# Latent attention core: the score banks seeded by ScalarE and VectorE copies in place of TensorE products

## The chip, the cores and the metric

The kernel is a whole four-layer decoder on one core of a Trainium2 chip. The metric is the device time of the program in microseconds, as the median of the runs. The engines are TensorE (PE; its weight loads are PEld), VectorE (DVE), ScalarE (ACT), GpSimd (POOL) and SyncE (SP), which issues the DMAs; each runs its own instructions in the order in which they are written and waits on semaphores.

## The reference, cut to what matters

Of twelve sublayers the change touches one, the latent cross-attention of layer 2. Its queries come from the 512 decoder positions of each of 4 batches, its keys and values from 1024 context positions and those 512 together, in 16 heads of 64.

```python
def _L2_xattn_ref(x, latents, ln_m_g, ln_m_b, ln_l_g, ln_l_b, Wq, Wkv, Wout):
    ...
    q = lat @ Wq
    kv_input = jnp.concatenate([x, lat], axis=1)
    kv = kv_input @ Wkv
    ...
    q, k, v = (split_heads(q), split_heads(k), split_heads(v))
    dots = jnp.einsum('bhid,bhjd->bhij', q, k) * scale
    attn = jax.nn.softmax(dots, axis=-1)
    out = jnp.einsum('bhij,bhjd->bhid', attn, v)
```

The softmax is taken with the row maximum subtracted before the exponential; the maximum comes from products of operands rounded to bf16, and any value near it serves, since it cancels in the division.

## The kernel before

`latent_core_stage` does the attention itself. A group is two heads of one batch, so there are 8 groups in a batch and 32 in all; `for_groups` runs the first two unrolled, then a loop of three turns of eight groups, then the last six. In a group the 1536 keys are cut into 12 tiles of 128 (`nkt`), and a step i works on one tile of keys against all 512 queries of both heads. TensorE's order in a group is written by hand, two steps at a time:

- `scores` for i and for i+1. Each puts, for both heads, a product of a row of ones with the row of negated maxima (L1017, the seed) and then the fp32 product of keys and queries (L1019) into two PSUM banks. The banks from `B0` on are four: two for even steps, two for odd ones, so `scores` of step i waits for the exponential of step i-2.
- one `pass_a` (L999): the rounded bf16 products of the next group, whose maxima VectorE takes (L1123). There are 12 a group, and they run ahead: those that step i issues for the next group are number i+4 on, and the last four belong to the group after it. Their two banks are single, so each waits for VectorE to have read the one before it.
- `weigh` (L1029) for i-2 and i-1: values times exponentials, into the bank `ACC`.
- a second `pass_a`.

`turn` (L1006) transposes the next group's row maxima at i = 8, and `spread` (L1039) sums the last group's totals over the partitions at i = 2. ScalarE takes the exponential of both heads in one instruction of 128x1024 (L1102), copies the sums of the last group after step 1 (L1089) and rounds the operands of the group after next after step 5 (L1082, L1083). VectorE takes the maxima, at i = 8 turns the transposed maxima into two bf16 parts (`negate`: L1132, L1133, L1135), adds a third of one head's exponentials (L1142) and inverts the last group's sums (L1150). GpSimd adds the other exponentials (L1188, L1193) and multiplies by the inverse (L1198). SyncE's queue holds, in each group, a wait for the last group's values products, the load of the next values (L955) and of the operands three groups on (L951, L952), and `row`: a wait for `negate` and four small DMAs that put the parts into the strips of `max_row` (L965).

Of the kernel before, what the change touches and what calls it, by code (L numbers as in the profile page):

```python
# [23 lines left out]
F32 = mybir.dt.float32  # L24
# [7 lines left out]
P = 128  # L32
# [826 lines left out]
def latent_core_stage(k, q_store, k_store, values, nk, scale, att_of):  # L859
# [26 lines left out]
    with ExitStack() as held:  # L886
        def sb(what, shape, dt=F32):
            return held.enter_context(nc.sbuf_tensor(f"lc_{what}", shape, dt))
# [5 lines left out]
        max_row, ones_row = sb("max_row", [P, 2, nq], BF16), sb("ones_row", [P, P], BF16)  # L894
# [4 lines left out]
        negative, max_parts = sb("negative", [SLOTS, P]), sb("max_parts", [SLOTS, ROW_PARTS, P], BF16)  # L899
        (rounded, a_ready, a_taken, row_done, turned, high_made, row_made, row_in, s_ready, exp_done, pv_done, acc_copied,  # L900
         added_by_pool, added_by_vector, sums_ready, inverted, normed, set_up, *more) = held.enter_context(k.stage(
             "rounded", "a_ready", "a_taken", "row_done", "turned", "high_made", "row_made", "row_in", "s_ready", "exp_done", "pv_done",
             "acc_copied", "added_by_pool", "added_by_vector", "sums_ready", "inverted", "normed", "set_up",
# [42 lines left out]
        def _(sync):  # L946
# [11 lines left out]
            def row(b, g):  # L958

                if before(b, g, 1):  # L960
                    sync.wait_ge(set_up, 1)
                sync.wait_ge(row_made, at(b, g, 1, 1))
                for j in range(HEADS):
                    for p in range(ROW_PARTS):
                        sync.dma_start(max_row[j * D + p:j * D + p + 1, g % 2, :].rearrange("o (i t) -> o i t", t=P),  # L965
                                       max_parts[j * nqt:(j + 1) * nqt, p, :]).then_inc(row_in, 16)
# [22 lines left out]
        def _(pe):  # L989
# [18 lines left out]
            def scores(b, g, i):  # L1008

                if i == 0:  # L1010
                    pe.wait_ge(loaded[g % RING], loads_done(b, g))
                    pe.wait_ge(row_in, 16 * HEADS * ROW_PARTS * at(b, g, 1, 1))
                if not (before(b, g, 1) and i < 2):
                    pe.wait_ge(exp_done, at(b, g, nkt, i - 1))
                out = [k.ps[:, B0 + (i % 2) * HEADS + j, 0:nq] for j in range(HEADS)]
                for j in range(HEADS):
                    nc.tensor.matmul(out[j], ones_row[strip(j), :], max_row[strip(j), g % 2, :], start=True, stop=False)  # L1017
                for j in range(HEADS):
                    mm = nc.tensor.matmul(out[j], k_tile[g % RING][strip(j), i * P:(i + 1) * P], q_tile[g % RING][strip(j), :], start=False, stop=True)  # L1019
                mm.then_inc(s_ready, 1)  # L1020
# [12 lines left out]
            def spread(b, g, negated):  # L1033

                pe.wait_ge(row_made, negated)
# [5 lines left out]
                mm.then_inc(sums_ready, 1)  # L1041

            for p in range(NP):
                pass_a(0, 0, p)
# [3 lines left out]
            pe.wait_ge(set_up, 1)  # L1048
# [28 lines left out]
        def _(act):  # L1077
# [12 lines left out]

            round_operands(0, 0)
            round_operands(0, 1)

            def group(b, g):
                for i in range(nkt):
                    if not (before(b, g, 1) and i < TILES):
# [16 lines left out]
        def _(dve):  # L1113
            nc.vector.memset(ones_row[:], 1.0)
            nc.vector.memset(max_row[:], 0.0).then_inc(set_up, 1)

# [11 lines left out]
            def negate(b, g):  # L1128
                dve.wait_ge(turned, at(b, g, 1, 1))
                if not before(b, g, 1):  # L1130
                    dve.wait_ge(row_in, 16 * HEADS * ROW_PARTS * at(b, g, 1, 0))
                nc.vector.tensor_scalar(max_parts[:, 0, :], k.ps[0:SLOTS, SIDE, 0:P], -1.0, None, ALU.mult).then_inc(high_made, 1)  # L1132
                nc.vector.tensor_scalar(negative[:, :], k.ps[0:SLOTS, SIDE, 0:P], -1.0, None, ALU.mult).then_inc(high_made, 1)  # L1133
                dve.wait_ge(high_made, at(b, g, 2, 2))
                nc.vector.tensor_tensor(max_parts[:, 1, :], negative[:, :], max_parts[:, 0, :], ALU.subtract).then_inc(row_made, 1)  # L1135
# [1818 lines left out]
```

## Time and profile before

| | us |
|---|---|
| median of 3 runs | 5089.19 |
| lowest and highest | 5087.92, 5093.08 |
| the profiled execution, its own time | 5096.03 |
| its span | 5094.2 |
| first product of the latent core to its last inverse | 2851 to 3811 |
| TensorE busy, whole span | 4249.6 (83%) |
| VectorE, ScalarE, GpSimd busy, whole span | 2899.7, 2381.9, 1406.3 |

The latent core is about a fifth of the span. Busy shares of the whole span say nothing of it, since eleven other sublayers are in them; it is read by stretches between 2851 and 3811 us. The granted clock is a mean over a stretch: 1.00 is 2.4 GHz and 0.50 is 1.2 GHz.

### The profile page before, as it was taken

The numbers are of one execution on the slowest core, as the hardware profiler recorded it, in microseconds if no ns is written. First come the engines' busy times: TensorE is split into PE (matmuls) and PEld (weight loads), VectorE is DVE, ScalarE is ACT, GpSimd is POOL, SyncE is SP. The second block draws the span as 40 slices with busy tenths as digits, with TensorE's granted clock in tenths as the row PEclk, the third lists the DMA queues.
The fourth block names the chain that finished last, engine by engine and source line by source line (L and its number), as shares of the span: only waits on it lengthen the run. The fifth ranks groups of instructions, "written<-read, shape, count | busy, mean of one in ns | idle before, by whom it ended". The sixth has DMA issues, their size and how long they took to land. (4 is left out here: it accounts for less than half of the span.)

```text
span 5094.2 us, 69502 instructions
## 1 busy us (share of the span) xinstructions
PE 4249.6 (83%) x20468; PEld 2010.7 (39%) x20468; DVE 2899.7 (57%) x6454; ACT 2381.9 (47%) x4625; POOL 1406.3 (28%) x1234
## 2 busy tenths in 40 slices
PE   7679755698688996896969799999988978589986
PEld 5323445395542323562324233333335644212223
DVE  4458474303558883005850477878753355388866
ACT  4447331243234774332743354545542245359992
POOL 3112141212030001112110287878880312200001
PEclk9769877799887997996989899999998989679998
DMA  8645112453073333665433312112111254823321
GB/s 299 152 103 131 31 45 34 161 192 125 14 254 76 95 80 106 249 203 171 107 79 151 108 59 74 59 59 73 59 36 37 78 154 99 300 74 97 101 70 36
DMA packets 462044, 564.36 MB, mean 111 GB/s; under 512 B 80868, under 2 KB 363988, under 8 KB 448772
## 3 DMA queue, kind: packets, MB, share of 16 engines
q1 hardware_dynamic: 454272, 525.35, 34.4%
q0 software_dynamic: 6384, 32.61, 2.1%
q8 instruction: 138, 2.26, 0.2%
q10 hardware_dynamic: 1068, 2.66, 0.2%
q14 instruction: 182, 1.49, 0.1%
HBM read 346.04 MB, written 200.54 MB: 107 GB/s over the span
## 5 line engine op out<-in xcount | busy, mean ns | idle before, releaser
L1193 POOL TENSOR_TENSOR lc_totals<-lc_totals,lc_weights 128x1024 f32<-128x1024 f32 (+1 forms) x320 | 625.6, 1955 | 163.8 <-DVE lc_totals L1142 131.1
L1102 ACT ACTIVATE lc_weights<-ps 128x1024 f32<-128x1024 f32 x384 | 393.2, 1024 | 439.8 <-PE ps L1019 426.8
L1123 DVE TENSOR_REDUCE lc_part_max<-ps 128x2 f32<-128x1024 f32 x384 | 466.1, 1214 | 203.6 <-PE ps L999 202.2
L1019 PE MATMUL ps<-lc_q,lc_k 64*128 64x512 f32 x1536 | 396.7, 595 | 0.0
L1029 PE MATMUL ps<-lc_weights,lc_v 128*64 128x512 f32 x1536 | 372.3, 606 | 0.0
L734 DVE TENSOR_REDUCE l1x_core_part_max<-ps 128x1 f32<-128x512 f32 x512 | 316.8, 681 | 77.7 <-PE ps L558 77.4
L730 DVE CUSTOM_DVE_ANT_0 l3x_core_unused<-ps,l3x_core_mask_q 128x512 f32<-128x512 f32 x512 | 330.7, 686 | 6.2 <-DVE l3x_core_row_max L738 4.9
L693 ACT ACTIVATE l3x_core_weights<-ps 128x512 f32<-128x512 f32 x512 | 325.0, 688 | 7.9 <-PE ps L626 7.5
L693 ACT ACTIVATE l1x_core_weights<-ps 128x512 f32<-128x512 f32 x512 | 266.1, 604 | 86.9 <-PE ps L626 86.8
L676 ACT ACTIVATE ps<-l3x_core_mask_k 128x512 f32<-128x512 f32 x384 | 268.1, 698 | 30.0 <-DMA l3x_core_mask_k<-in_mask_k 30.0
L558 PE MATMUL ps<-l3x_core_k,l3x_core_q 96*128 96x512 bf16 x512 | 214.8, 420 | 53.1 <-DVE l3x_core_part_max L730 38.1
L218 POOL TENSOR_TENSOR proj_parts<-proj_rest,proj_parts 128x512 bf16<-128x512 f32 x112 | 136.0, 1217 | 337.0 <-ACT proj_parts L169 336.5
L558 PE MATMUL ps<-l1x_core_k,l1x_core_q 96*128 96x512 bf16 x512 | 209.7, 412 | 19.1 <-DMA l1x_core_k<-k_parts 15.2
L626 PE MATMUL ps<-l3x_core_q,l3x_core_k 99*128 99x512 bf16 x512 | 198.6, 394 | 19.0 <-ACT ps L676 18.0
L626 PE MATMUL ps<-l1x_core_q,l1x_core_k 99*128 99x512 bf16 x512 | 192.3, 386 | 6.1 <-ACT l1x_core_weights L693 6.1
L1319 DVE SCALAR_TENSOR_TENSOR rn_z<-ps,rn_z 128x256 f32<-128x256 f32 x112 | 45.6, 415 | 262.3 <-PE ps L1290 194.9
L189 ACT ACTIVATE proj_value<-ps 128x256 f32<-128x256 f32 (+2 forms) x224 | 103.6, 475 | 177.7 <-PE ps L159 123.2
L734 DVE TENSOR_REDUCE l2a_core_row_max<-ps 128x1 f32<-128x512 f32 x256 | 158.4, 679 | 46.8 <-PE ps L558 46.7
L1019 PEld LDWEIGHTS ps<-lc_q,lc_k 64*128 64x128 f32 x1536 | 147.9, 189 | 94.2 <-issue 64.8
L734 DVE TENSOR_REDUCE pyr_core_row_max<-ps 128x1 f32<-128x512 f32 x256 | 158.2, 679 | 46.7 <-PE ps L558 46.6
L999 PE MATMUL ps<-lc_k_round,lc_q_round 64*128 64x512 bf16 x768 | 151.8, 392 | 32.7 <-DVE lc_part_max L1123 20.5
L1029 PEld LDWEIGHTS ps<-lc_weights,lc_v 128*64 128x64 f32 x1536 | 93.5, 136 | 212.1 <-issue 120.3
(468 smaller groups left out, 8673.0 us busy)
## 6 DMA issues: line engine op xcount, KB each, us to landing
cf_w<-in_L1f_w SPq DMA_DIRECT2D x32, 1024.0 KB, 7.8
values<-proj_value SPq DMA_DIRECT2D x112, 256.0 KB, 3.1
lc_k<-latent_k SPq DMA_DIRECT2D x32, 768.0 KB, 6.7
lc_v<-latent_values SPq DMA_DIRECT2D x32, 768.0 KB, 5.0
k_parts<-proj_parts SPq DMA_DIRECT2D x56, 384.0 KB, 2.6
latent_k<-feed_staged SPq DMA_DIRECT2D x64, 256.0 KB
latent_values<-feed_staged SPq DMA_DIRECT2D x64, 256.0 KB
q_parts<-proj_parts SPq DMA_DIRECT2D x40, 384.0 KB, 2.9
```

Of the source, the lines that this page charges most:

```text
L558: mm = nc.tensor.matmul(out, q_stack[r][0:rows_a, j, qs], k_stack[r][0:rows_a, j, keys], start=True, stop=not causal)
L626: mm = nc.tensor.matmul(out, k_stack[r][0:rows_b, j, ks], q_stack[r][0:rows_b, j, qs], start=not seeded, stop=not (causal or seeded), skip ...
L676: nc.scalar.activation(k.ps[:, B0 + (g * NS + s) % B_BANKS, 0:nq], seed, ACT.Copy).then_inc(filled, 1)
L693: nc.scalar.activation(weights[:, (g * NS + s) % WEIGHTS, qs], k.ps[:, B0 + (g * NS + s) % B_BANKS, qs], ACT.Exp, scale=scale).then_inc(ex ...
L730: nc.vector.tensor_tensor_reduce(unused[:, n % 2, :], scores, mask_q[:, qi, keys], 1.0, -3.0e38, ALU.add, ALU.max, out).then_inc(a_taken, 1)
L734: nc.vector.reduce_max(out, scores, AX).then_inc(a_taken, 1)
L999: mm = nc.tensor.matmul(k.ps[:, A0 + j, :], q_round[strip(j), g % 2, qs], k_round[strip(j), g % 2, keys], start=True, stop=True)
L1019: mm = nc.tensor.matmul(out[j], k_tile[g % RING][strip(j), i * P:(i + 1) * P], q_tile[g % RING][strip(j), :], start=False, stop=True)
L1029: mm = nc.tensor.matmul(k.ps[strip(j), ACC, 0:nq], v_tile[g % V_RING][:, i, strip(j)], weights[:, i % TILES, j, :], start=i == 0, stop=i = ...
L1102: nc.scalar.activation(weights[:, i % TILES, :, :], k.ps[:, B0 + (i % 2) * HEADS:B0 + (i % 2 + 1) * HEADS, 0:nq], ACT.Exp, scale=scale).th ...
L1123: nc.vector.reduce_max(own, k.ps[:, A0:A0 + HEADS, :], AX).then_inc(a_taken, 1)
L1193: nc.gpsimd.tensor_tensor(total, total, own, ALU.add).then_inc(added_by_pool, 1)
```

## The change

The banks are no longer seeded by TensorE. ScalarE (10 of 12 steps) and VectorE (steps 3 and 9) copy the negated maxima, as fp32, into the banks of a step before its products, and the products add to what stands there. For that each partition needs all 1024 negated maxima of the two heads: `tops`, 4 KB on each of 128 partitions, 512 KB a group. SyncE makes it in two DMAs, one after the other: the 8x128 negated maxima go to DRAM, SyncE waits until they have landed, and a second DMA reads the 4 KB back to every partition. VectorE's `negate` shrinks to one instruction. Four products at the start, whose results nothing reads, open the banks, so that later products add to them.

```diff
-    ROW_PARTS = 2
+    VECTOR_FILLS = (3, 9)
+    SCALAR_FILLS = tuple(i for i in range(nkt) if i not in VECTOR_FILLS)
...
+                sync.wait_ge(negated, at(b, g, 1, 1))
+                sync.dma_start(max_rows[g % 2, :, :], negative[:, g % 2, :]).then_inc(row_stored, 16)
+                sync.wait_ge(row_stored, 16 * at(b, g, 1, 1))
+                sync.dma_start(tops[:, g % 2, :, :].rearrange("p j n -> p (j n)"),
+                               max_rows[g % 2, :, :].rearrange("s t -> (s t)").partition_broadcast(P)).then_inc(row_in, 16)
...
-                    pe.wait_ge(row_in, 16 * HEADS * ROW_PARTS * at(b, g, 1, 1))
-                if not (before(b, g, 1) and i < 2):
-                    pe.wait_ge(exp_done, at(b, g, nkt, i - 1))
+                if i in VECTOR_FILLS:
+                    pe.wait_ge(filled_by_vector, at(b, g, len(VECTOR_FILLS), VECTOR_FILLS.index(i) + 1))
+                else:
+                    pe.wait_ge(filled, at(b, g, len(SCALAR_FILLS), SCALAR_FILLS.index(i) + 1))
                 out = [k.ps[:, B0 + (i % 2) * HEADS + j, 0:nq] for j in range(HEADS)]
                 for j in range(HEADS):
-                    nc.tensor.matmul(out[j], ones_row[strip(j), :], max_row[strip(j), g % 2, :], start=True, stop=False)
-                for j in range(HEADS):
-                    mm = nc.tensor.matmul(out[j], k_tile[g % RING][strip(j), i * P:(i + 1) * P], q_tile[g % RING][strip(j), :], start=False, stop=True)
+                    mm = nc.tensor.matmul(out[j], k_tile[g % RING][strip(j), i * P:(i + 1) * P], q_tile[g % RING][strip(j), :], start=False, stop=False,
+                                          skip_group_check=True)
...
+            def fill(b, g, i):
+
+                if i == 0:
+                    act.wait_ge(row_in, 16 * at(b, g, 1, 1))
+                nc.scalar.activation(k.ps[:, B0 + (i % 2) * HEADS:B0 + (i % 2 + 1) * HEADS, 0:nq], tops[:, g % 2, :, :], ACT.Copy).then_inc(filled, 1)
...
+                    ahead = (*later(b, g, (i + 2) // nkt), (i + 2) % nkt)
+                    if ahead[2] in SCALAR_FILLS and exists(*ahead[:2]):
+                        act.wait_ge(exp_done, at(b, g, nkt, i + 1))
+                        fill(*ahead)
...
+            def fill(b, g, i):
+                dve.wait_ge(row_in, 16 * at(b, g, 1, 1))
+                dve.wait_ge(exp_done, at(b, g, nkt, i - 1))
+                nc.vector.tensor_copy(k.ps[:, B0 + (i % 2) * HEADS:B0 + (i % 2 + 1) * HEADS, 0:nq], tops[:, g % 2, :, :]).then_inc(filled_by_vector, 1)
...
                     if exists(*pair[:2]):
                         maxima(*pair)
+                    if i + 2 in VECTOR_FILLS:
+                        fill(b, g, i + 2)
```

ScalarE at the passage from one group to the next. Of before: eight exponentials in a row, six of them of the group that ends and two of the one that begins, then the copy of the sums, and four more.

```order
L1102 ACTIVATE lc_weights<-ps 128x1024 x8
L1089 ACTIVATE lc_sums<-ps 128x512
L1102 ACTIVATE lc_weights<-ps 128x1024 x4
L1082 ACTIVATE lc_q_round<-lc_q3 128x512
L1083 ACTIVATE lc_k_round<-lc_k3 128x1536
```

Of after, the same passage (L1114 is now the exponential, L1098 the fill): the exponential of step 10 of the group that ends, the fill for step 0 of the next group, the exponential of step 11, the fill for step 1, and so on; step 3 has no fill here.

```order
L1114 ACTIVATE lc_weights<-ps 128x1024
L1098 ACTIVATE ps<-lc_tops 128x1024
L1114 ACTIVATE lc_weights<-ps 128x1024
L1098 ACTIVATE ps<-lc_tops 128x1024
L1114 ACTIVATE lc_weights<-ps 128x1024
L1098 ACTIVATE ps<-lc_tops 128x1024
L1114 ACTIVATE lc_weights<-ps 128x1024
L1092 ACTIVATE lc_sums<-ps 128x512
L1114 ACTIVATE lc_weights<-ps 128x1024
L1098 ACTIVATE ps<-lc_tops 128x1024
```

The first fill of a group now stands between two exponentials of the group before it.

VectorE around steps 7 and 8 of a group, of before: the last maxima of the next group, their row maxima, the first maxima of the group after it, and the three instructions of `negate`.

```order
L1123 TENSOR_REDUCE lc_part_max<-ps 128x2
L1126 TENSOR_REDUCE lc_row_max<-lc_part_max 128x8
L1123 TENSOR_REDUCE lc_part_max<-ps 128x2
L1132 TENSOR_SCALAR lc_max_parts<-ps 8x128
L1133 TENSOR_SCALAR lc_negative<-ps 8x128
L1135 TENSOR_TENSOR lc_max_parts<-lc_negative,lc_max_parts 8x128
L1123 TENSOR_REDUCE lc_part_max<-ps 128x2
```

Of after: L1136 takes the maxima, and L1150 is the fill for step 9.

```order
L1136 TENSOR_REDUCE lc_part_max<-ps 128x2
L1139 TENSOR_REDUCE lc_row_max<-lc_part_max 128x8
L1150 COPY ps<-lc_tops 128x1024
L1136 TENSOR_REDUCE lc_part_max<-ps 128x2
L1145 TENSOR_SCALAR lc_negative<-ps 8x128
L1136 TENSOR_REDUCE lc_part_max<-ps 128x2
```

The fill has come between the row maxima and the next maxima, and two small instructions have gone from `negate`.

## Rows read from the trace of the kernel before

**Rows 1.** Busy time by stretch: us, PE, PEld, DVE, ACT, POOL busy, PEclk, DMA, GB/s
```profile
3480.00:3600.00 120.00, 120.00 (x633) 41.34 (x631) 98.85 (x106) 61.17 (x62) 98.52 (x52) 1.00 0.19 62
```

**Rows 2.** Timeline of PE and ACT, one pair of steps: start us, us, engine, line
```profile
3104.12 0.38 PE L1017 MATMUL ps<-lc_max_row,lc_ones_row 64*128 64x512 bf16 x2
...
3104.33 1.02 PE L1019 MATMUL ps<-lc_q,lc_k 64*128 64x512 f32 x4
...
3105.19 0.38 PE L1017 MATMUL ps<-lc_max_row,lc_ones_row 64*128 64x512 bf16 x2
...
3105.41 2.10 ACT L1102 ACTIVATE lc_weights<-ps 128x1024 f32<-128x1024 f32 x2 [2.66 <-PE ps L1019]
...
3106.27 0.38 PE L999 MATMUL ps<-lc_k_round,lc_q_round 64*128 64x512 bf16 x2
...
3106.57 1.94 PE L1029 MATMUL ps<-lc_weights,lc_v 128*64 128x512 f32 x8
...
3108.67 0.38 PE L1017 MATMUL ps<-lc_max_row,lc_ones_row 64*128 64x512 bf16 x2
```

**Rows 3.** Timeline of ACT: the copy of the sums in four groups running
```profile
3113.19 0.60 ACT L1089 ACTIVATE lc_sums<-ps 128x512 f32<-128x512 f32 x1 [1.14 <-PE ps L1029]
...
3141.58 0.60 ACT L1089 ACTIVATE lc_sums<-ps 128x512 f32<-128x512 f32 x1 [1.14 <-PE ps L1029]
...
3176.33 0.60 ACT L1089 ACTIVATE lc_sums<-ps 128x512 f32<-128x512 f32 x1 [1.88 <-PE ps L1029]
...
3204.99 0.60 ACT L1089 ACTIVATE lc_sums<-ps 128x512 f32<-128x512 f32 x1 [1.14 <-PE ps L1029]
```

**Rows 4.** Timeline around the turn of the maxima, steps 7 to 9 of a group
```profile
3101.18 0.18 DVE L1126 TENSOR_REDUCE lc_row_max<-lc_part_max 128x8 f32<-128x24 f32 x1
...
3101.51 0.38 PE L999 MATMUL ps<-lc_k_round,lc_q_round 64*128 64x512 bf16 x2
...
3101.93 1.23 DVE L1123 TENSOR_REDUCE lc_part_max<-ps 128x2 f32<-128x1024 f32 x1 [0.57 <-PE ps L999]
...
3103.07 0.27 DVE L1132 TENSOR_SCALAR lc_max_parts<-ps 8x128 bf16<-8x128 f32 x1
```

**Rows 5.** A copy into PSUM by ScalarE in another attention: duration min/median/max ns
```profile
L676 ACT ACTIVATE ps<-l3x_core_mask_k x384: 583/674/946, 4459.2 to 4977.7; 128x512 f32<-128x512 f32 x192
```

**Rows 6.** A copy into PSUM by VectorE there: duration min/median/max ns
```profile
L758 DVE COPY ps<-l3x_core_mask_k x128: 676/695/696, 4459.2 to 4975.7; 128x512 f32<-128x512 f32 x128
```

**Rows 7.** Groups by line, page part 5: busy us, mean ns, idle us before
```profile
L1102 ACT ACTIVATE lc_weights<-ps 128x1024 f32<-128x1024 f32 x384 | 393.2, 1024 | 439.8 <-PE ps L1019 426.8
L1123 DVE TENSOR_REDUCE lc_part_max<-ps 128x2 f32<-128x1024 f32 x384 | 466.1, 1214 | 203.6 <-PE ps L999 202.2
...
L734 DVE TENSOR_REDUCE l1x_core_part_max<-ps 128x1 f32<-128x512 f32 x512 | 316.8, 681 | 77.7 <-PE ps L558 77.4
```

**Rows 8.** Timeline of SP: stores to DRAM, each with the DMA behind its wait
```profile
4982.73 0.60 SPq L1242 DMA_DIRECT2D sums_of_weights<-l3x_att  x1
4984.98 0.34 SPq L1244 DMA_DIRECT2D rn_dense<-sums_of_weights  x1
4987.36 0.33 SPq L1246 DMA_DIRECT2D inverse_sums<-rn_dense_inverse  x1
4988.84 1.73 SPq L1249 DMA_DIRECT2D rn_inverse_sums<-inverse_sums  x4
```

**Rows 9.** DMA issues: KB each, median us from issue to landing
```profile
la_rows<-in_L2x_rows SPq DMA_DIRECT2D x1, 512.0 KB, 3.8
```

**Rows 10.** Timeline of PE at the first turn of the latent loop
```profile
3168.94 0.61 PE L1017 MATMUL ps<-lc_max_row,lc_ones_row 64*128 64x512 bf16 x2 [3.34 <-issue]
```

**Rows 11.** Busy time by stretch, the columns of rows 1: behind that turn
```profile
3168.00:3176.00 8.00, 7.06 (x22) 2.33 (x22) 2.15 (x2) 2.05 (x2) 3.40 (x3) 0.57 0.02 5
```

**Rows 12.** Timeline of PE in a stage whose groups take 10 us
```profile
202.57 0.39 PE L626 MATMUL ps<-pyr_coarse_q,pyr_coarse_k 99*128 99x256 bf16 x1 [1.62 <-DMA pyr_coarse_q<-pyr_coarse_max_parts]
```

**Rows 13.** Busy time by stretch: one group of that stage
```profile
202.00:212.00 10.00, 8.24 (x65) 4.25 (x65) 5.61 (x18) 5.27 (x17) 1.22 (x3) 0.67 0.46 111
```

More of the change, by code:

```diff
@@ L893, in latent_core_stage @@
         q_round, k_round = sb("q_round", [P, 2, nq], BF16), sb("k_round", [P, 2, nk], BF16)
-        max_row, ones_row = sb("max_row", [P, 2, nq], BF16), sb("ones_row", [P, P], BF16)
+        tops = sb("tops", [P, 2, HEADS, nq])
+        max_rows = nc.dram_tensor("lc_max_rows", [2, SLOTS, P], F32, kind="Internal").ap()
         weights = sb("weights", [P, TILES, HEADS, nq])
@@ L898, in latent_core_stage @@
         part_max, row_max = sb("part_max", [P, 2, SLOTS, nwide]), sb("row_max", [P, 2, SLOTS])
[L899 to L903, printed above, removed]
+        negative = sb("negative", [SLOTS, 2, P])
+        (rounded, a_ready, a_taken, row_done, turned, negated, row_stored, row_in, s_ready, exp_done, pv_done, acc_copied,
+         added_by_pool, added_by_vector, sums_ready, inverted, normed, opened, filled, filled_by_vector, *more) = held.enter_context(k.stage(
+             "rounded", "a_ready", "a_taken", "row_done", "turned", "negated", "row_stored", "row_in", "s_ready", "exp_done", "pv_done",
+             "acc_copied", "added_by_pool", "added_by_vector", "sums_ready", "inverted", "normed", "opened", "filled", "filled_by_vector",
              *(f"loaded{r}" for r in range(RING)), *(f"v_loaded{r}" for r in range(V_RING))))
@@ L958, in row @@
             def row(b, g):
-                if before(b, g, 1):
-                    sync.wait_ge(set_up, 1)
-                sync.wait_ge(row_made, at(b, g, 1, 1))
-                for j in range(HEADS):
-                    for p in range(ROW_PARTS):
-                        sync.dma_start(max_row[j * D + p:j * D + p + 1, g % 2, :].rearrange("o (i t) -> o i t", t=P),
-                                       max_parts[j * nqt:(j + 1) * nqt, p, :]).then_inc(row_in, 16)
+                sync.wait_ge(negated, at(b, g, 1, 1))
[3 more added lines that the diff above has]
+                               max_rows[g % 2, :, :].rearrange("s t -> (s t)").partition_broadcast(P)).then_inc(row_in, 16)
             load_group(0, 0)
@@ L1011, in scores @@
                     pe.wait_ge(loaded[g % RING], loads_done(b, g))
-                    pe.wait_ge(row_in, 16 * HEADS * ROW_PARTS * at(b, g, 1, 1))
-                if not (before(b, g, 1) and i < 2):
-                    pe.wait_ge(exp_done, at(b, g, nkt, i - 1))
+                if i in VECTOR_FILLS:
+                    pe.wait_ge(filled_by_vector, at(b, g, len(VECTOR_FILLS), VECTOR_FILLS.index(i) + 1))
+                else:
+                    pe.wait_ge(filled, at(b, g, len(SCALAR_FILLS), SCALAR_FILLS.index(i) + 1))
                 out = [k.ps[:, B0 + (i % 2) * HEADS + j, 0:nq] for j in range(HEADS)]
                 for j in range(HEADS):
-                    nc.tensor.matmul(out[j], ones_row[strip(j), :], max_row[strip(j), g % 2, :], start=True, stop=False)
-                for j in range(HEADS):
-                    mm = nc.tensor.matmul(out[j], k_tile[g % RING][strip(j), i * P:(i + 1) * P], q_tile[g % RING][strip(j), :], start=False, stop=True)
+                    mm = nc.tensor.matmul(out[j], k_tile[g % RING][strip(j), i * P:(i + 1) * P], q_tile[g % RING][strip(j), :], start=False, stop=False,
+                                          skip_group_check=True)
                 mm.then_inc(s_ready, 1)
@@ L1031, in weigh, with spread @@
                 mm.then_inc(pv_done, 1)
-            def spread(b, g, negated):
-                pe.wait_ge(row_made, negated)
+            def spread(b, g, last_negated):
+                pe.wait_ge(negated, last_negated)
                 pe.wait_ge(added_by_pool, at(b, g, nkt, nkt))
@@ L1041, in spread @@
                 mm.then_inc(sums_ready, 1)
+            pe.wait_ge(rounded, 2)
+            for i in range(2 * HEADS):
+                nc.tensor.matmul(k.ps[:, B0 + i, 0:nq], k_round[:, 0, 0:P], q_round[:, 0, :], start=True, stop=False,
+                                 skip_group_check=True).then_inc(opened, 1)
             for p in range(NP):
@@ L1047, in _ @@
                 pass_a(0, 1, p)
-            pe.wait_ge(set_up, 1)
             def group(b, g):
@@ L1089, in copy_sums @@
                 nc.scalar.activation(sums[:, g % 2, :], k.ps[:, ACC, 0:nq], ACT.Copy).then_inc(acc_copied, 1)
+            def fill(b, g, i):
+                if i == 0:
+                    act.wait_ge(row_in, 16 * at(b, g, 1, 1))
+                nc.scalar.activation(k.ps[:, B0 + (i % 2) * HEADS:B0 + (i % 2 + 1) * HEADS, 0:nq], tops[:, g % 2, :, :], ACT.Copy).then_inc(filled, 1)
             round_operands(0, 0)
             round_operands(0, 1)
+            act.wait_ge(opened, 2 * HEADS)
+            for i in range(2):
+                fill(0, 0, i)
             def group(b, g):
@@ L1113, in _ @@
         def _(dve):
-            nc.vector.memset(ones_row[:], 1.0)
-            nc.vector.memset(max_row[:], 0.0).then_inc(set_up, 1)
             def maxima(b, g, p):
@@ L1129, in negate @@
                 dve.wait_ge(turned, at(b, g, 1, 1))
[L1130 to L1135, printed above, removed]
+                if not before(b, g, 2):
+                    dve.wait_ge(row_stored, 16 * at(b, g, 1, -1))
+                nc.vector.tensor_scalar(negative[:, g % 2, :], k.ps[0:SLOTS, SIDE, 0:P], -1.0, None, ALU.mult).then_inc(negated, 1)
+            def fill(b, g, i):
+                dve.wait_ge(row_in, 16 * at(b, g, 1, 1))
+                dve.wait_ge(exp_done, at(b, g, nkt, i - 1))
+                nc.vector.tensor_copy(k.ps[:, B0 + (i % 2) * HEADS:B0 + (i % 2 + 1) * HEADS, 0:nq], tops[:, g % 2, :, :]).then_inc(filled_by_vector, 1)
             def add_weights(b, g, i):
```

## Prediction, made before the changed kernel had run

> **What bounds the kernel now.** The latent core is read alone, since nothing outside it changes. First the busy time by stretch: in 120 us of its steady part TensorE is busy for 120.00 at a granted clock of 1.00, which is 2.4 GHz, while VectorE has 98.85 and ScalarE 61.17 [rows 1]. Then the timeline of a pair of steps, which shows what a busy TensorE is doing: it goes without a hole from seed to scores to maxima products to values products, and the pair, from its first seed at 3104.12 to the next pair's at 3108.67, takes 4.55 us [rows 2]. Then the repeat of one instruction, ScalarE's copy of the sums: 3113.19 to 3141.58, so a group takes 28.39 us [rows 3]. Six pairs are 27.3; `spread` and `turn` are the rest. The core is bound by TensorE's queue, and the change takes work from exactly that queue. The question is whether TensorE can still run without a hole when each pair of banks must be freed, filled by another engine, and handed back.
>
> **What goes.** A seed costs TensorE 3104.33 - 3104.12 = 0.21 us [rows 2]: 12 x 0.21 = 2.5 us a group. If nothing else changed, a pair would take 4.55 - 0.42 = 4.13. `negate` loses two small VectorE instructions, and SyncE issues two DMAs in place of four; neither ends a wait of TensorE now, so they give nothing but an earlier row, which is counted below. The four products that open the banks run once, while TensorE waits for VectorE's first maxima, and are left at nothing.
>
> **The fills by VectorE, steps 3 and 9.** VectorE's fill for step 3 stands behind the maxima of the product that TensorE issues just ahead of the scores of step 2. The start of such a product to that of its maxima is 3101.93 - 3101.51 = 0.42, and the next VectorE instruction starts 1.14 later, at 3103.07 [rows 4]. So the fill starts 1.56 after the product. Its length is not in the latent core; the nearest row is a copy into PSUM of half the width, 695 ns [rows 6], and reading PSUM costs 681 at that width and 1214 at the full one [rows 7], so I take 1.23 us. It is done 2.8 after the product, 2.9 with the signal. TensorE would want the scores of step 3 after 0.21 + 0.86 = 1.07 (0.86 is scores to the next seed, 3104.33 to 3105.19 [rows 2]). It stands still for 1.8 us, and since its queue is in order, everything behind waits too. At step 9 the row maxima (0.18 [rows 4]) come first: 2.0. Together 3.8 us a group, where two seeds cost 0.4. The bounds: at the 0.695 of the half width the two stalls are 2.7; if GpSimd's use of SBUF holds the copy up, which no copy of the trace shows (its longest is 696 [rows 6]), I allow one us more for each, 5.8.
>
> At half the width copy and reduction differ by 14 ns [rows 6, 7]: nothing in the trace shows a VectorE copy into PSUM at a faster pace than its reading of PSUM. The Trainium skill gives a reason in "VectorE: DVE Perf Modes", section "Why PSUM operands drop a tier": a copy with any operand in PSUM runs fp32 at 1x, while between SBUF tiles it would run at 2x. At the 2x pace the fill would be near 0.7 us and the sum about 33 us lower over the stage; by the rule it is 1.23, and the trace agrees.
>
> **The row of maxima.** The first fill of a group stands on ScalarE between the exponentials of steps 10 and 11 of the group before, and waits for `tops`. I walk it with the times of [rows 2, 4]. The one `negate` instruction starts at 3103.07 and ends at 3103.34. SyncE then stores, waits and broadcasts. Of a store and the wait behind it the trace has 1.48 (4987.36 to 4988.84) and 2.25 (4982.73 to 4984.98) [rows 8]; the nearest broadcast, also 4 KB to each of 128 partitions, lands after 3.8 [rows 9]. With 0.1 to start, that is 5.4 to 6.2; I take 5.8, hence 3109.1. The exponential of step 10 starts 1.08 after its scores (3104.33 to 3105.41 [rows 2]), without the seed at 3105.2, and ends at 3106.2. ScalarE stands still for 2.9 us; the fill ends at 3110.1. TensorE would want those scores at 3104.12 + 4.13 = 3108.25: a hole of 1.9. Behind the fill the exponential of step 11 and the fill for step 1 take 2.1, to 3112.2, where TensorE wants step 1 at 3111.1: 1.2 more with the signal. Together 3.2 us a group; with 5.4 it is 2.8, and with 7.0, as other loads may press, 4.4. In the kernel before, this row had until the next group's scores, at 3108.67 + 4.55 = 3113.2, and no exponential stood behind it.
>
> **ScalarE's queue.** A fill of 128x1024: copies of half the width take 583 to 674 ns [rows 5], the exponential of the full one 1024 [rows 7], so 1.03 (up to 1.12). A pair with two fills is 2 x (1.02 + 1.03) and four waits of 0.05, 4.3 us, more than the 4.13 that TensorE would like; in the pair with the rounding (0.62 + 1.47 less an overlap, 2.0) it is 6.3, which is 2.1 over. VectorE's two fills, and the holes already counted, give some back. I take 1.8 a group, from 0.5 to 2.5.
>
> **The sum.** -2.5 + 3.8 + 3.2 + 1.8 = +6.3 us a group, so 34.7 in place of 28.4. Over 31 passages (32 groups, of which the first has its row made ahead of the loop): +195.
>
> **The clock.** At the first turn of the loop TensorE stood still for 3.34 us [rows 10], and then was granted 0.57 over the next 8 [rows 11]: the lower level, 1.2 GHz, for most of it. That passage took 3176.33 - 3141.58 = 34.75, the next 28.66 [rows 3]: 6.6 over twice the usual, of which 3.3 is the hole and 3.3 the clock. A shorter hole does it too: in a stage with one hole of 1.62 us in a group of 10 us [rows 12] the mean is 0.67 [rows 13]. The changed kernel has holes of 1.8, 2.0 and 1.9 us in each group, where TensorE was full. I expect one fall to 1.2 GHz a group; it costs at most 3.3, and some hides in the waits that follow, so 2.0: 31 x 2.0 = +62.
>
> The profiled execution took 5096.03, 0.13% above the median of 5089.19. 5096 + 195 + 62 = 5353; less the 7 us between them, 5346.
>
> **The rivals.**
> (a) The holes leave the clock alone: they are shorter than the 3.34 of [rows 10]. Then 5346 - 62 = 5284. Speaks against it: [rows 12, 13].
> (b) The clock falls twice a group, or stays low: 5.3 in place of 2.0, +102, so 5448. For it: a TensorE that waits a quarter of the time. Against: at the low clock its work fills the holes.
> (c) The row is in time. It would have to land 2.9 us after `negate`; one DMA alone takes more in [rows 9]. Then 3.2 a group less, 5247, or 5185 without the clock.
> (d) Faster. By busy time there is room: ScalarE's exponentials have 439.8 us of idle time before them and gain 320 fills of 1.03 = 330; VectorE has 203.6 and gains 64 of 1.23 = 79 [rows 7]. If the fills are hidden, TensorE keeps the 2.5 us: 5089 - 32 x 2.5 = 5009. It decides at one place: the fill for step 3 must be done 1.07 us after the product ahead of step 2, and VectorE is still taking that product's maxima then. Only if the maxima were taken well ahead could it be.
> (e) Gain and loss cancel, say with (c) and VectorE's fills half hidden: within 0.2%.
>
> **How the numbers follow.** Forecast as reasoned 0.44; (a) 0.22; (b) 0.16; (c) 0.12; (d) 0.04; (e) 0.02. Some 0.2% of 5089, 10 us, is what a measurement can tell. Faster 0.04, same 0.02, slower 0.94. The range takes in (a), the upper half of (c), and (b) to its middle, with the bounds of fills and row (31 x 1 us each way): 5220 to 5450.
>
> **What would show it.** TensorE's products of scores idle before steps 3 and 9 with VectorE's copy as the releaser, about 1.8 and 2.0 us each, and before step 0 with ScalarE's copy; ScalarE's first fill of a group waits for the DMA of `tops`, about 3 us, 31 times; the copy of the sums repeats every 36 to 37 us; the granted clock of 120 us of the core falls under 0.9. If the copy of the sums repeats at 26 us, (d) holds and I have misread which queue the fills stand in; if the first fill finds its row there, (c); if the clock stays at 1.00 with a repeat of 34.7, (a). A VectorE copy much over 1.23 us would show that GpSimd holds it up.

## The result and the profile after

The changed kernel takes 5262.1 us (median of 4 runs, 5254.48 to 5267.41), the kernel before 5088.56: 173.5 us more, a ratio of 1.0337, with a 95% interval from 1.0324 to 1.0351. The forecast was 5346 in a range of 5220 to 5450, with 0.94 on slower. The sign and the range held; the size was 84 us too high, and the time lies nearer to rival (a), 5284, than to the forecast. The profiled execution took 5265.96.

First the groups by line of the changed kernel, in the columns of [rows 7], and the landing time of the broadcast, in those of [rows 9]:

```profile
L1136 DVE TENSOR_REDUCE lc_part_max<-ps 128x2 f32<-128x1024 f32 x384 | 463.1, 1206 | 544.0 <-PE ps L999 540.5
...
L1018 PE MATMUL ps<-lc_q,lc_k 64*128 64x512 f32 x1536 | 426.3, 650 | 164.5 <-DVE ps L1150 113.5
L1114 ACT ACTIVATE lc_weights<-ps 128x1024 f32<-128x1024 f32 x384 | 389.9, 1015 | 255.9 <-PE ps L1018 244.7
...
L1098 ACT ACTIVATE ps<-lc_tops 128x1024 f32<-128x1024 f32 x320 | 328.8, 1028 | 73.7 <-DMA lc_tops<-lc_max_rows 63.8
...
L1150 DVE COPY ps<-lc_tops 128x1024 f32<-128x1024 f32 x64 | 78.0, 1218 | 6.2 <-ACT lc_weights L1114 6.2
...
lc_tops<-lc_max_rows SPq DMA_DIRECT2D x32, 512.0 KB, 3.6
```

TensorE's scores (L1018), which before stood behind a seed and never waited, now have 164.5 us of idle time before them, most of it ended by VectorE's fill, L1150. ScalarE's 320 fills found their room, as rival (d) had counted: its exponentials wait 256 us for the scores where they waited 440 [rows 7]. The idle time before VectorE's maxima grew from 203.6 [rows 7] to 544.0, so neither of the two engines that fill is short of time. The durations that were taken from half-width rows were right: 1028 ns for ScalarE's fill (1.03 foreseen), 1218 for VectorE's (1.23), 3.6 us for the broadcast (3.6 to 3.8).

The waits of the latent core, 2890 to 3980, first TensorE's, then ScalarE's: us in total, times, longest.

```profile
PE ps L1018 <- DVE ps L1150: 113.5, 64, 2.7
PE ps L1018 <- ACT ps L1098: 46.9, 78, 3.1
...
ACT ps L1098 <- DMA lc_tops<-lc_max_rows: 35.3, 23, 2.6
```

TensorE waits 64 times for VectorE, 1.8 us each, and 78 times for ScalarE, 0.6 each. ScalarE waits for the row 23 times, 1.5 us each.

The timeline of one group (columns as in [rows 2]) around step 3, around step 9, and from `negate` to the first scores of the next group:

```profile
3091.91 0.39 PE L999 MATMUL ps<-lc_k_round,lc_q_round 64*128 64x512 bf16 x2
3092.14 1.02 PE L1018 MATMUL ps<-lc_q,lc_k 64*128 64x512 f32 x4
3092.34 1.23 DVE L1136 TENSOR_REDUCE lc_part_max<-ps 128x2 f32<-128x1024 f32 x1 [0.37 <-PE ps L999]
3093.49 1.22 DVE L1150 COPY ps<-lc_tops 128x1024 f32<-128x1024 f32 x1
3094.76 1.13 PE L1018 MATMUL ps<-lc_q,lc_k 64*128 64x512 f32 x4 [1.60 <-DVE ps L1150]
...
3109.90 0.18 DVE L1139 TENSOR_REDUCE lc_row_max<-lc_part_max 128x8 f32<-128x24 f32 x1
3109.99 1.22 DVE L1150 COPY ps<-lc_tops 128x1024 f32<-128x1024 f32 x1
3111.27 2.08 PE L1018 MATMUL ps<-lc_q,lc_k 64*128 64x512 f32 x4 [2.05 <-DVE ps L1150]
...
3114.95 0.27 DVE L1145 TENSOR_SCALAR lc_negative<-ps 8x128 f32<-8x128 f32 x1
3115.25 0.30 SPq L963 DMA_DIRECT2D lc_max_rows<-lc_negative  x1
...
3116.48 0.33 SPq L965 DMA_DIRECT2D lc_tops<-lc_max_rows  x1
...
3120.30 1.03 ACT L1098 ACTIVATE ps<-lc_tops 128x1024 f32<-128x1024 f32 x1 [1.86 <-DMA lc_tops<-lc_max_rows]
...
3121.38 1.13 PE L1018 MATMUL ps<-lc_q,lc_k 64*128 64x512 f32 x4 [0.75 <-ACT ps L1098]
```

The two holes of VectorE's fills are 1.60 and 2.05 us, where 1.8 and 2.0 were foreseen, and they are made as foreseen: product of the maxima, its maxima, the fill, the scores. The scores behind the second hole take 2.08 us in place of 1.13: TensorE's clock fell to the lower level there. Four stretches of 4 us show it, with PE's busy time and its granted clock behind it:

```profile
3110.00:3114.00 4.00, 2.73 (x7) 0.64 0.01 2
3114.00:3118.00 4.00, 4.00 (x19) 0.93 0.12 44
3118.00:3122.00 4.00, 3.25 (x18) 1.00 0.29 88
3122.00:3126.00 4.00, 3.13 (x17) 1.00 0.00 0
```

A passage is the time from one copy of the sums to the next, so the time that one group takes. Two passages that follow each other take 33.25 and 34.11 us where before it was 28.39 [rows 3]:

```profile
3615.03 0.60 ACT L1092 ACTIVATE lc_sums<-ps 128x512 f32<-128x512 f32 x1 [0.41 <-PE ps L1029]
3648.28 0.60 ACT L1092 ACTIVATE lc_sums<-ps 128x512 f32<-128x512 f32 x1 [0.37 <-PE ps L1029]
3682.39 0.60 ACT L1092 ACTIVATE lc_sums<-ps 128x512 f32<-128x512 f32 x1 [0.37 <-PE ps L1029]
```

The second passage has a fall of the clock in it, the first none. Without the last passage, in which the core runs out of work, there are 8 without a fall, median 33.5, 21 with one, median 34.4, and one of 40.4 that holds a turn of the loop and two falls. Over all 31 passages the mean went from 28.59 to 34.13 us; 31 x 5.54 = 172 us is the whole loss but for 2 us. The mean clock of the core (columns as in [rows 1]) is 0.93; a stretch of before from the same start had 0.99.

```profile
2882.00:3960.00 1078.00, 911.10 (x3887) 268.60 (x3885) 716.61 (x738) 766.15 (x781) 712.60 (x373) 0.93 0.20 65
```

### The profile page after: what moved, and what is told of

Read it like the earlier page. It is cut to its first block and busy times, and to the rows that moved or that the text cites. A ratio compares the mean times of both kernels' runs of the same rounds, so it can differ in the third digit from the quotient of the medians.

```text
span 5264.2 us, 68574 instructions
## 1 busy us (share of the span) xinstructions
PE 4264.9 (81%) x19704; PEld 1970.1 (37%) x19704; DVE 2913.7 (55%) x6452; ACT 2694.4 (51%) x4945; POOL 1393.5 (26%) x1234
## 5 line engine op out<-in xcount | busy, mean ns | idle before, releaser
L1136 DVE TENSOR_REDUCE lc_part_max<-ps 128x2 f32<-128x1024 f32 x384 | 463.1, 1206 | 544.0 <-PE ps L999 540.5
L1018 PE MATMUL ps<-lc_q,lc_k 64*128 64x512 f32 x1536 | 426.3, 650 | 164.5 <-DVE ps L1150 113.5
L1114 ACT ACTIVATE lc_weights<-ps 128x1024 f32<-128x1024 f32 x384 | 389.9, 1015 | 255.9 <-PE ps L1018 244.7
L1029 PE MATMUL ps<-lc_weights,lc_v 128*64 128x512 f32 x1536 | 399.0, 643 | 0.0
L1098 ACT ACTIVATE ps<-lc_tops 128x1024 f32<-128x1024 f32 x320 | 328.8, 1028 | 73.7 <-DMA lc_tops<-lc_max_rows 63.8
L1018 PEld LDWEIGHTS ps<-lc_q,lc_k 64*128 64x128 f32 x1536 | 137.6, 196 | 325.0 <-DVE ps L1150 167.3
```

The lines of the kernel that those rows point to most:

```text
L1029: mm = nc.tensor.matmul(k.ps[strip(j), ACC, 0:nq], v_tile[g % V_RING][:, i, strip(j)], weights[:, i % TILES, j, :], start=i == 0, stop=i = ...
L1098: nc.scalar.activation(k.ps[:, B0 + (i % 2) * HEADS:B0 + (i % 2 + 1) * HEADS, 0:nq], tops[:, g % 2, :, :], ACT.Copy).then_inc(filled, 1)
L1114: nc.scalar.activation(weights[:, i % TILES, :, :], k.ps[:, B0 + (i % 2) * HEADS:B0 + (i % 2 + 1) * HEADS, 0:nq], ACT.Exp, scale=scale).th ...
L1136: nc.vector.reduce_max(own, k.ps[:, A0:A0 + HEADS, :], AX).then_inc(a_taken, 1)
```

## The experiments

The repeat of the copy of the sums is the finest measure: it is taken in each kernel as the median of the passages in whose granted clock no fall stands, and, where there are enough, of those with one fall. The last two passages, in which the work runs out, stay out of the medians; counts of passages leave out the last one only. A ratio is taken against the kernel before as it ran beside that kernel, at 5088.68, 5090.99 or 5089.79 us. The theory is the prediction's: each term of its sum is a cost of its own, and TensorE's holes come from where the fills stand. The main rival was that the loss is occupancy: the engines that fill are too full, wherever the fills stand.

**Each term alone.** All twelve fills on ScalarE, in the changed kernel:

```
-    VECTOR_FILLS = (3, 9)
+    VECTOR_FILLS = ()
```

> All 12 fills of a group on ScalarE, none on VectorE. The places theory (VectorE's fills of steps 3 and 9 stand behind maxima that have only just been asked for, so TensorE waits 1.8 and 2.3 us): both holes go and ScalarE gets two fills of 1.03 back; by the walk with the durations of the trace of after the repeat of a group falls by about 2.7 us, x31 = -83, near 5180. The occupancy theory (ScalarE has too much to do, 25.6 us of work in 34.3): two more fills add 2.06 us a group, +64, near 5326.

Measured: 5152.7 us, ratio 1.0125 [1.0085, 1.0164], and a repeat of 30.35. The 12 fills on ScalarE cost much less than 10 there and 2 on VectorE, where occupancy had 5326: it falls as a cause of this part of the loss. The time is 27 us below the 5180 of the places theory, since the repeat fell by more than the 2.7 expected and fewer passages have a fall of the clock, 8 of 30. So VectorE's fills are worth 33.47 - 30.35 = 3.1 a group without a fall. ScalarE now waits for the row for 60.8 us in 30 waits, where it was 35.3 in 23 with VectorE's holes ahead of it:

```profile
ACT ps L1098 <- DMA lc_tops<-lc_max_rows: 60.8, 30, 4.2
```

The row's wait taken away: the fills copy a tile of zeros, and the row is still stored and broadcast.

```
-                nc.scalar.activation(k.ps[...], tops[:, g % 2, :, :], ACT.Copy)
+                nc.scalar.activation(k.ps[...], flat[:, :, :], ACT.Copy)
...
-                nc.vector.tensor_copy(k.ps[...], tops[:, g % 2, :, :])
+                nc.vector.tensor_copy(k.ps[...], flat[:, :, :])
```

> The fills, where after has them, copy a tile of zeros set once, so no fill waits for the row of maxima; the row is still made and broadcast, and nothing reads it. The maxima are thus not subtracted. The row theory (the first fill of a group waits 1.9 us for the broadcast, and TensorE has holes of 0.75 and 0.87 us behind it): the repeat falls by 1.5 to 2.3 us, x31 = -46 to -72, near 5190 to 5216. If the row is hidden behind other waits: within 10 us of 5262.

Measured: 5206.6 us, 1.0231 [1.0201, 1.026]; repeat 31.32 without a fall of the clock, 33.2 with one. That lies in the 5190 to 5216 that were expected if the row costs, and the row is worth 33.47 - 31.32 = 2.15 a group.

Both at once, `VECTOR_FILLS = ()` and the tile of zeros:

> Both at once: zeros in place of the maxima, with no wait for the row, and all fills on ScalarE. What is left is ScalarE's queue alone, a fill and an exponential for each step one behind the other and the rounding. Places theory: the walk gives a repeat of 28.8 us, +0.4 over before, near 5089 + 12 = 5101, so that even then nothing is won. Occupancy theory: ScalarE's work of 12 x (1.02 + 1.03 + 0.1) + 2.6 = 28.4 us a group, the same within 10 us; if the two losses found so far are independent, -83 and -60 on 5262 give 5119.

Measured: 5081.1 us in 8 runs, 0.9979 [0.9969, 0.9989]; repeat 28.24. The two differences come out again: 30.35 - 28.24 = 2.11 for the row, 31.32 - 28.24 = 3.08 for VectorE's fills. In passages without a fall the terms add. In device time they add less well: VectorE's fills are worth 5262.1 - 5152.7 = 109 us beside the row and 5206.6 - 5081.1 = 126 without it, and the row 56 us beside VectorE's fills and 72 without them, though the two runs with 5152.7 as their median are 15 us apart. Device time also holds the falls of the clock, which are in 22 of 30 passages of the changed kernel, in 16 without the row, in 8 without VectorE's fills, and with neither only in the 2 that hold a turn of the loop. The kernel was 20 us faster than expected: the fills by ScalarE and the seeds taken away almost cancel.

To part those two, the kernel before without its seeds and without fills:

```
-                for j in range(HEADS):
-                    nc.tensor.matmul(out[j], ones_row[strip(j), :], max_row[strip(j), g % 2, :], start=True, stop=False)
                 for j in range(HEADS):
-                    mm = nc.tensor.matmul(out[j], k_tile..., q_tile..., start=False, stop=True)
+                    mm = nc.tensor.matmul(out[j], k_tile..., q_tile..., start=True, stop=True)
```

> The kernel before without the seeds: the scores open the banks themselves, and the maxima are not subtracted. It measures what the seeds cost, the gain that the change could have had. If TensorE's queue is the bound and each seed is 0.21 us of it: 32 x 2.5 = 80 us less than before, 5009. If VectorE's maxima, which TensorE waits for in some pairs, take over as the bound: less than that, 5030 to 5050.

Measured: 5052.9 us, 0.9925 [0.9905, 0.9945]; repeat 27.18. The twelve seeds are 2.5 us of TensorE's time, but are worth 1.2. The rest turns into idle time: of 120 us of the core, TensorE is now busy for 115.42, where it was busy for all 120.00 [rows 1].

```profile
3480.00:3600.00 120.00, 115.42 (x551) 37.59 (x551) 96.21 (x107) 61.46 (x66) 105.76 (x54) 1.00 0.20 62
```

It waits for VectorE's maxima, which free the banks of the maxima products. In 900 us of the core the products and their weight loads wait in this kernel, and the weight loads then in the kernel before,

```profile
PE ps L999 <- DVE lc_part_max L1121: 25.0, 42, 1.0
PEld ps L999 <- DVE lc_part_max L1121: 252.7, 320, 1.8
```
```profile
PEld ps L999 <- DVE lc_part_max L1123: 175.6, 325, 1.3
```

where the products themselves had waited 0.5 us. The weight loads' 77 us more are not lost time one for one: in the kernel before, TensorE hardly stood still beside 175.6 us of them. From this kernel to the one with ScalarE's fills and no row it is 28.24 - 27.18 = +1.06, the price of ScalarE's fills, less whatever the shorter `negate` gives, which that kernel has and this one has not. In that kernel TensorE waits for ScalarE for 38.1 us in 64 waits, two a group:

```profile
PE ps L1020 <- ACT ps L1098: 38.1, 64, 0.9
```

**The place of VectorE's fills.** VectorE fills steps 2 and 8 in place of 3 and 9. A fill then stands behind the maxima of the product that TensorE issues ahead of the values products, not of the one right ahead of the scores:

```
-    VECTOR_FILLS = (3, 9)
+    VECTOR_FILLS = (2, 8)
```

> As many fills on VectorE as after, two a group, but for steps 2 and 8 in place of 3 and 9: TensorE wants those 2 us later after the product whose maxima VectorE takes first. Places theory: the two holes shrink from 1.8 and 2.3 us to about 0.5 each, in part given back to ScalarE's queue: the repeat falls by 1.3 us, -40, near 5222. Occupancy theory, or a VectorE copy that is slow by itself: no change, 5262 within 10.

Measured: 5195.8 us, 1.0209 [1.018, 1.0239]; repeat 31.2 without a fall, 33.3 with one. The scores wait 24.2 us for VectorE in place of 113.5:

```profile
PE ps L1018 <- ACT ps L1098: 59.6, 60, 3.4
PE ps L999 <- DVE lc_part_max L1136: 36.9, 57, 1.9
PE ps L1018 <- DVE ps L1150: 24.2, 51, 0.6
```

It was 26 us faster than the 5222 expected by place, and far from the 5262 expected by occupancy. The same engine, copy and count cost 31.2 - 30.35 = 0.8 a group here and 3.1 at steps 3 and 9: the price is one of place. What is left has moved to the next product of the maxima, which now waits for VectorE too.

VectorE's fills at 3 and 9 without any by ScalarE: the kernel before, with its seeds at the ten other steps and a broadcast of the maxima beside its own row.

```
+    FILLS = (3, 9)
...
-                if not (before(b, g, 1) and i < 2):
+                if i not in FILLS and not (before(b, g, 1) and i < 2):
                     pe.wait_ge(exp_done, at(b, g, nkt, i - 1))
+                if i in FILLS:
+                    pe.wait_ge(filled, at(b, g, len(FILLS), FILLS.index(i) + 1))
+                    ...
...
                         maxima(*pair)
+                    if i + 2 in FILLS:
+                        dve.wait_ge(tops_in, 16 * at(b, g, 1, 1))
+                        dve.wait_ge(exp_done, at(b, g, nkt, i + 1))
+                        nc.vector.tensor_copy(k.ps[...], tops[:, g % 2, :, :]).then_inc(filled, 1)
```

> The kernel before with VectorE's copies for steps 3 and 9 alone; the ten other steps are seeded by TensorE, and ScalarE has no fill. Theory (VectorE's fill is late because it stands behind the maxima of the product ahead of the scores, whatever ScalarE does): two holes of 1.6 to 2.0 us before steps 3 and 9, less two seeds, so 28.38 + 3.8 - 0.4 = 31.8 a group, about 5195 us. Rival (in the changed kernel VectorE's fills cost 3.9 a group only because a filled ScalarE leaves no slack to win the holes back): one part of each hole is won back, the repeat is 29.5 to 30.3, about 5135.

Measured: 5226.6 us, 1.0264 [1.0234, 1.0293]; repeat 32.1 without a fall of the clock, 33.5 with one. The first is the theory's 31.8 within 0.3. The rival, that a ScalarE without fills wins part of the holes back, falls: with ScalarE busy for 44% of this core (440.54 of 1000 us) in place of 71% (766.15 of 1078) the two fills cost 3.7, not less. The expectation had left out the clock, which falls in 20 of 30 passages here at 1.4 each; that is most of the 31 us by which 5195 was short.

**The clock.** The changed kernel with products whose result nothing reads, in both holes: 5 before the scores of step 3, 8 before those of step 9, into a bank that is idle then.

```
+            def keep_warm(n):
+                for _ in range(n):
+                    nc.tensor.matmul(k.ps[:, SIDE, 0:nq], k.ident_bf[:, :], warm[:, :], start=True, stop=True)
...
+                    if i == 2:
+                        pe.wait_ge(negated, at(b, g, 1, 1))
+                        keep_warm(5)
+                    if i == 8:
+                        if not before(b, g, 1):
+                            pe.wait_ge(inverted, at(b, g, QUARTERS, 0))
+                        keep_warm(8)
```

> Inside the holes of steps 3 and 9 TensorE gets 5 and 8 bf16 products of 128x512 into the bank SIDE, which nobody reads then; each is about 0.22 us, so 1.1 in a hole of 1.6 to 1.8 and 1.7 in one of 2.1 to 2.3. The waits stay as they are. Clock theory (groups with a fall to 1.2 GHz repeat after 34.3 to 34.7 us, those without after 33.1): the granted clock of the core goes from 0.93 to over 0.98 and the repeat to 33.1, 25 of 31 groups x 1.3 = -33, near 5229. If the fall costs nothing, because the waits hide it: 5262 or a little more.

Measured: 5255.5 us (5249.41 to 5261.57), 1.0327 [1.0293, 1.036], an interval that covers the changed kernel's ratio. The products did fill the holes, as the timeline shows, and the clock did rise:

```profile
3502.05 1.25 PE L1046 MATMUL ps<-lc_warm,ident_bf 128*128 128x512 bf16 x5
3502.44 1.22 DVE L1165 COPY ps<-lc_tops 128x1024 f32<-128x1024 f32 x1
3503.71 1.13 PE L1019 MATMUL ps<-lc_q,lc_k 64*128 64x512 f32 x4 [0.41 <-DVE ps L1165]
...
3518.11 1.90 PE L1046 MATMUL ps<-lc_warm,ident_bf 128*128 128x512 bf16 x8
3518.96 1.23 DVE L1165 COPY ps<-lc_tops 128x1024 f32<-128x1024 f32 x1
3520.24 1.13 PE L1019 MATMUL ps<-lc_q,lc_k 64*128 64x512 f32 x4 [0.23 <-DVE ps L1165]
```
```profile
2882.00:3960.00 1078.00, 975.04 (x4329) 297.50 (x4327) 730.73 (x743) 774.44 (x789) 716.73 (x377) 0.98 0.20 65
```

The clock of the core is 0.98 in place of 0.93, and 21 of its passages have no fall, median 33.5, which is the changed kernel's own. So a passage without a fall gains nothing from these products and loses nothing to them. The 33 us that the clock's theory expected of the whole did not come: the two medians are 7 us apart, which two runs cannot tell from nothing. What a fall costs is therefore read from the passages of the changed kernel: 34.4 - 33.5 = 0.9 (the few falls left here cost 1.6, among more products). A fall costs more in kernels with fewer other waits: 33.2 - 31.32 = 1.9 without the row, 33.5 - 32.1 = 1.4 with VectorE's fills alone. Two passages of the kernel without the row, next to each other, columns as in [rows 1]:

```profile
3240.67:3273.89 33.22, 28.75 (x127) 8.53 (x127) 23.78 (x25) 24.65 (x26) 23.13 (x13) 0.95 0.21 72
3273.89:3305.21 31.32, 27.14 (x127) 8.25 (x127) 23.48 (x25) 24.64 (x26) 23.13 (x13) 1.00 0.24 76
```

With 127 products in each, PE is busy 1.6 us longer at a clock of 0.95, and the passage is 1.9 longer: nothing of the fall is hidden there.

In the changed kernel about half of it is. Two passages next to each other, the first with a fall, and in each what TensorE waited for ScalarE and ScalarE for the row:

```profile
3024.44:3058.95 34.51, 30.05 (x127) 8.78 (x127) 23.41 (x25) 24.56 (x25) 23.13 (x13) 0.90 0.21 69
3058.95:3092.03 33.08, 27.35 (x127) 8.16 (x127) 23.13 (x25) 24.57 (x26) 22.89 (x13) 1.00 0.21 72
```
```profile
PE ps L1018 <- ACT ps L1098: 0.8, 2, 0.4
ACT ps L1098 <- DMA lc_tops<-lc_max_rows: 0.4, 1, 0.4
```
```profile
PE ps L1018 <- ACT ps L1098: 2.0, 3, 0.9
ACT ps L1098 <- DMA lc_tops<-lc_max_rows: 1.9, 1, 1.9
```

PE is busy 2.7 us longer in the first, but the passage is only 1.4 longer: TensorE comes later to the next group, by then the row has all but landed, and 1.2 us of its waits are gone. A passage of the kernel without the row with a clock of 0.90 too takes 34.27:

```profile
3010.51:3044.78 34.27, 30.08 (x127) 8.78 (x127) 23.49 (x25) 24.64 (x25) 23.15 (x13) 0.90 0.22 70
```

Against 31.32 with neither, such a fall alone costs 2.9 us, the row alone 1.8 and both together 3.2: they hide each other.

**The row, by its place.** The kernel before with ScalarE's fills for steps 2 to 11 and seeds for 0 and 1, so that the broadcast has a pair of steps more:

```
+    FILLS = tuple(range(2, nkt))
...
+                    if i + 2 in FILLS:
+                        if i + 2 == FILLS[0]:
+                            act.wait_ge(tops_in, 16 * at(b, g, 1, 1))
+                        act.wait_ge(exp_done, at(b, g, nkt, i + 1))
+                        nc.scalar.activation(k.ps[...], tops[:, g % 2, :, :], ACT.Copy).then_inc(filled, 1)
```

> The kernel before with ScalarE's copies for steps 2 to 11 and TensorE's seeds for steps 0 and 1. The row is still stored and broadcast, but its first reader is the fill for step 2, which stands a whole pair of steps later than the fill for step 0. Theory (the row's 2.2 us a group in the changed kernel are its lateness before the fills of steps 0 and 1): the wait is gone, the copy of the sums repeats at the 28.24 of the kernel with no row and ScalarE's fills alone, plus at most 0.3 for two seeds, 28.3 to 28.5; about 5087 us. Rival (the price lies in the transfers themselves, or in ten fills on ScalarE of which one waits for the row wherever it stands): a repeat near the 30.4 of the kernel with all twelve fills on ScalarE, about 5150.

Measured: 5106.7 us in 8 runs, 1.0033 [1.0022, 1.0045]; repeat 29.21, between the theory's 28.3 to 28.5 and the rival's 30.4. Of the row's 2.1 us, 1.1 goes when its first reader stands later. ScalarE's wait for it falls from 60.8 us to 7.1:

```profile
ACT ps L1122 <- DMA lc_tops<-lc_max_rows: 7.1, 19, 0.5
```

The other 1.0 over the kernel with no row at all is not the late row of the changed kernel, since the wait is gone. One passage of this kernel and one of the kernel with no row part it in two:

```profile
3321.14:3350.41 29.27, 27.49 (x129) 8.55 (x129) 22.10 (x25) 24.19 (x26) 22.70 (x13) 1.00 0.26 81
3306.25:3334.49 28.24, 26.87 (x127) 8.21 (x125) 21.50 (x23) 26.27 (x28) 23.21 (x13) 1.00 0.26 84
```

TensorE is busy 0.6 us longer, of which the two seeds are 2 x 0.21, and idle 0.4 us longer. Candidates for the idle part are ScalarE's wait (7.1 us over some 30 groups, 0.2 each), the seeds' own wait for the row of parts (4.3 us in 22 waits, none in the kernel before), and the two VectorE instructions of the old `negate`, which this kernel keeps and the other doesn't have. They weren't measured apart.

**A version faster than both.** If what hurts is a fill that comes late, fewer of them may keep some of the gain. The kernel just above, with fills for every second step only, so that one fill and not two stands in ScalarE's queue in a pair of steps, and seeds for the others:

```
+    FILLS = (2, 4, 6, 8, 10)
```

> The kernel before with ScalarE's fills for steps 2, 4, 6, 8 and 10 alone; steps 0 and 1 and all odd ones keep their seeds by TensorE, from the row of parts as before. The first fill then needs the broadcast 10 us after negate, and each fill is done 2.2 us or more before TensorE wants the bank. If it is the places of the fills that cost, and not the copies: 5 x 0.21 = 1.05 us a group less, -33, near 5056. If any copy between the exponentials delays the values products or the next scores: 5089 or slower.

Measured: 5068.0 us (5062.72 to 5074.42, 4 runs), 0.9952 [0.9935, 0.9968]: 23 us faster than the kernel before, and 12 short of what was expected. The repeat is 27.8, half way to the 27.18 of no seeds at all, and TensorE stays nearly full at the full clock:

```profile
3480.00:3600.00 120.00, 119.32 (x604) 40.04 (x604) 94.14 (x103) 83.62 (x88) 101.78 (x52) 1.00 0.30 95
```

## Why the prediction was right, and where it was off

The sum by terms, in us a group, as foreseen and as the differences of repeats measure them:

| term | foreseen | measured | from |
|---|---|---|---|
| seeds gone | -2.5 | -1.2 | 28.38 to 27.18 |
| ScalarE's queue | +1.8 | +1.06 | 27.18 to 28.24 |
| the row | +3.2 | +2.1 | 28.24 to 30.35 |
| VectorE's fills | +3.8 | +3.1 | 30.35 to 33.47 |
| falls of the clock | +2.0 | +0.6 | 0.9 in 21 of 30 passages |
| sum | +8.3 | +5.7 | |

Over 31 passages the right column is 31 x 5.7 = 177, against 173.5 measured. The four costs were foreseen 3.9 too high together and the gain 1.3 too high, so the two kinds of error cancelled in part: that the forecast missed by no more than 84 us is to that extent luck.

**VectorE's fills** were the largest term, and its mechanism is shown three ways: the chain of four rows in the trace, the fall from 3.1 to 0.8 when the fills move to steps 2 and 8, and 3.7 a group when nothing else is changed. The holes, 1.60 and 2.05, add up to 3.65, close to the 3.8. Beside the other losses the term is 3.1; which of them takes the 0.6 was not measured.

**The row** was over-sized by 1.1. The walk had the chain from `negate` to a landed broadcast at 5.8 us; in the group above it is from 3115.22 (the end of L1145) to 3120.30, 5.1. The store and its wait took 1.23 (3115.25 to 3116.48), below both values of [rows 8], 1.48 and 2.25; from there to the fill it was 3.82, as in [rows 9]. ScalarE stood still for 1.86 us there where 2.9 were foreseen, and the hole before step 0 was 0.75, not 1.9. With VectorE's fills gone, ScalarE waits for the row 2.0 us, 30 times, in place of 1.5, 23 times. In passages without a fall the row costs the same 2.1 with VectorE's fills and without them; it is the passages with a fall in which its lateness is hidden, and these come with VectorE's fills.

**ScalarE's queue** was over-sized by 0.7 and lay within its bounds, 0.5 to 2.5.

**The seeds** were the step that failed in the other direction. The prediction took all of TensorE's freed time for a gain: 12 x 0.21. The kernel without seeds shows 1.2, because VectorE's maxima end later than TensorE wants their banks, and the wait moved there. The first group of rows had the hint: VectorE was busy for 98.85 of 120 us, and the wait of the maxima products' weight loads for VectorE, 175.6 us in the kernel before, was in the trace and stands nowhere in the prediction. The hint was no proof, since beside the loads' 325 waits the products themselves had waited only once, for 0.5 us. For the same reason rival (d), 5009, was out of reach: the kernel with no seeds and no fills at all takes 5053.

**The clock** was the term furthest off, 1.4 of the 2.6 us between the two sums. That it would fall, about once a group and behind the holes, was right: 21 of 30 passages, and 0.93 over the core. The foreseen line "under 0.9" was not reached. What a fall costs was taken as 2.0 of a highest 3.3 from the turn of the loop, where TensorE had nothing to wait for afterwards. In the changed kernel 0.9 is left; the rest hides in the waits for the row, as the two passages above show: with a fall ScalarE waits 0.4 us for the row in place of 1.9. This was named as a possibility ("some hides in the waits that follow") and sized too high.

**What would show it**, by item: holes before steps 3 and 9 with VectorE's copy as releaser, right; a hole before step 0 with ScalarE's, right but less than half the size; ScalarE's wait for the DMA 31 times and 3 us, 23 times and 1.5; repeat of 36 to 37, 34.4. Rival (c), the row in time, is out by the waits. Rival (a) gave 5284 with a clock left alone: its number is nearer than the forecast's, but its mechanism is not what happened, since the clock does fall.

## What to carry to other kernels

Work taken from a full queue is worth only what the next resource behind it leaves: make the kernel that leaves the work out altogether first. Its time (here 5053, not 5009) is the mark for every way of doing that work elsewhere with the rest as it is, and no kernel here came below it. When an in-order engine is to hand back a buffer that another in-order engine waits for, write down what stands ahead of the hand-back in its queue: the same two copies cost 3.1 us a group behind one reduction and 0.8 behind another. And losses of one group hide each other, so terms that are sized one at a time come out too high together.

## What the runs showed of the hardware that was not expected

- With TensorE holes of 1.6 and 2.05 us in a group of 34, the granted clock fell to its lower level, 1.2 GHz, in 22 of 30 passages. One fall in a passage cost 0.9 us in the changed kernel (medians) and 1.9 in the kernel without the row's wait, where a passage with a mean clock of 0.90 took 2.9 us more (34.27 against 31.32).
- A copy of 128x1024 fp32 from SBUF into PSUM takes 1.03 us on ScalarE and 1.22 on VectorE. The Trainium skill's "VectorE: DVE Perf Modes", section "Why PSUM operands drop a tier", has a copy that touches PSUM at 1x in fp32; the 1218 ns agree, being the pace of the reduction that reads as much PSUM (1206 ns).
- A small store to DRAM, the wait for it, and the issue of the DMA behind that wait took 1.23 us (1.22 to 1.24 in the 32 groups of the changed kernel); the broadcast of 4 KB to each of 128 partitions landed after 3.6 (median).
